# Two of four output projection tiles moved in among the next batch's score rounds

## The chip, the cores and the metric

One Trainium2 chip; the kernel is one program on one of its cores. The core has a matrix engine (TensorE, in the profile PE, with its weight loads as PEld), a vector engine (VectorE, DVE), an activation engine (ScalarE, ACT), a general engine (GpSimd, POOL) and a queue processor that here issues all transfers (SyncE, SP). Each runs its own list of instructions in order and waits on semaphores for the others. The metric is the device time of one execution in microseconds; lower is better.

## The reference

Eight batches of x, 512 tokens by 512 features. All are independent of one another.

```python
def reference(x, Wq, Wk, Wv, Wo, w_fc, w_proj):        # x: (8, 512, 512) float32
    xn = layernorm(x)                                  # eps 1e-5
    s = attention(xn)      # q, k, v = xn @ W.T in 16 heads of 32; rotary embedding on q and k;
                           # causal softmax(q k / sqrt(32)) v; then ctx @ Wo.T
    g = silu(ffn(xn))      # bitlinear(xn, w_fc) to 2048, exact gelu, bitlinear(., w_proj) to 512;
                           # bitlinear: layer norm, absmax rounding, weights made ternary
    return x + s * g
```

## The kernel before

Each batch is treated by `body(b)`, which every engine has in its own version. Tiles of 128 tokens or features; PSUM has eight banks of 128 x 512 float32. Values that need more than 16 bits are held as a high and a low part, so a product takes three matmuls (`three_products`), or two where the weights are ternary.

PE goes through one batch in this order:

1. v: 4 token tiles of 12 matmuls (L378).
2. q and k: 4 pairs of heads' halves, 24 matmuls each (L378). DVE multiplies by the rotary tables (L998) and adds (L1004), ACT rounds the sums to the high part (L724), POOL takes the low part (L1202), and SP copies the parts to the score operands, six transfers a pair (L304, `stacks`). This rotary part ends some time after PE's last q or k matmul. After the last of it SP issues the load of the next batch's x (L308, `load_next`). ACT then loads the table for Gelu (L738).
3. The output projection of the batch before, `out_projection(b - 1)` (L381): 4 token tiles of 12 matmuls, ctx times Wo, in banks 6 and 7 by turns. Tiles 2 and 3 wait until DVE has scaled tiles 0 and 1 out of these banks (`scale_by_gate`, L952, the instruction at L958). DVE runs all four scalings after its rotary work and before block 0 of the up projection. POOL adds x to the scaled tile (`add_x`, L1196): tiles 0 and 1 after its rotary work, tiles 2 and 3 after additions 8 and 11 of the squares (`RESIDUAL_AFTER`). SP stores each tile (L269).
4. The up projection: 16 blocks f of 8 matmuls (L493), in banks 1, 0, 2 by turns (`UP_BANKS`). Per block ACT does Gelu (L752), DVE two passes for the high and low part (L1047, L1049), and ACT the square (L747), which frees the bank. ACT's order is Gelu f, then square f - 1. PE's block f waits for square f - 3 (L488). After blocks 5, 7, 9 and 11 DVE takes the statistics of one tile of the next batch's x (`token_statistics`, L928), which first wait for x (L927). POOL sums the squares (L1211).
5. The score rounds, 44 of them (`ROUNDS`), whose only purpose is each row's maximum and sum: 16 of one head with 512 keys, 16 of one head with 384, then 12 for the short rows, 4 heads by 128 keys or 2 by 256. A round's scores and its mask (L472, L479) go to one of the five banks 3, 4, 5, 2, 1; DVE takes the maximum (L1025), POOL makes the bias for Exp from it (L1218; DVE the first four), ACT takes Exp and its sum (L778), after which the bank is free for the fifth round behind. In the short rows' rounds DVE also shifts and sums (L1033, L1039). Rounds 0 to 2 stand behind up blocks 13 to 15.
6. Between the rounds PE does the down projection step by step: a generator `down()` (L504) yields after each matmul (L524; beside nearly each stands a one-column sum, L523), in banks 6 and 7 by turns, 32 steps per token tile. How many steps have been given after round r is the list `DOWN_AFTER_ROUND`: 0, 0, 11, 13, 16 and then in proportion to ACT's work, 84 by round 43. Then come steps up to 104, the transposes of the maxima (L547) and more down steps. ACT copies down tiles 0 and 1 out of their banks after rounds 15 and 35 (`KEEP_DOWN`, L785).
7. The maxima's rows go to the score operand by a transfer (L315), for which the second set of scores (L578) waits; then Exp of them in transposed form (L799), the weighing by v (L609), and the transposes of the next batch's tokens (L399).

For batch 0 there is no output projection. That of the last batch is done at the end (`last_out_projection`), and the change doesn't touch it.

```python
while given < DOWN_AFTER_ROUND[r]:
    next(downs)
    given += 1
```

Of the kernel before, what the change touches and what calls it, by code (L numbers as in the profile page):

```python
# [12 lines left out]
P = 128  # L13
NB, S, D = 8, 512, 512
# [3 lines left out]
NT = S // P  # L18
# [4 lines left out]
NG = H // GH  # L23
# [14 lines left out]
NR = len(ROUNDS)  # L38
# [10 lines left out]
NSQ = len(SQ_SLOTS)  # L49
RESIDUAL_AFTER = {8: 2, 11: 3}  # L50
STATS_AFTER = (5, 7, 9, 11)
# [8 lines left out]
DOWN_LEAD = (0, 0, 11, 13, 16)  # L60
DOWN_AFTER_ROUND = [DOWN_LEAD[r] if r < NSB else DOWN_LEAD[-1] + (DOWN_BESIDE_SCORES - DOWN_LEAD[-1]) * EXP_COLS[r - NSB] // EXP_COLS[-1]
                    for r in range(NR)]
KEEP_DOWN = tuple(1 + min(r for r in range(NR) if DOWN_AFTER_ROUND[r] >= (t + 1) * DOWN_MATMULS) for t in range(2))
DOWN_BESIDE_EXP = 12
# [6 lines left out]
def program(nc, x, w_q, w_k, w_v, w_o, w_fc, w_proj, rope_cos, rope_sin, out, norm_row):  # L71
    with ExitStack() as ctx:
# [264 lines left out]
        def _(pe):  # L337
# [43 lines left out]
            def out_projection(b):  # L381
                for t in range(NT):
                    if t == 0:
                        pe.wait_ge(ctx_lo, b * NG + NG)
                    if t >= 2:
                        pe.wait_ge(scaled_ready, b * NT + t - 1)
                    three_products(banks[:, 6 + t % 2, :],
                                   lambda a, r, c: (ctxT[:, a, c, t * P:(t + 1) * P], voT[:, 1, r, c, :]),
                                   NG, "o").then_inc(wo_ps, 1)

            def turn_tokens(b, t, first=False):
# [27 lines left out]
            def body(b, first=False, last=False):  # L419
# [62 lines left out]
                for f in range(FC):  # L482
                    if f < 2:
                        pe.wait_ge(v_ready, b * NT + 3 + f)
                    elif f < NUB:
                        pe.wait_ge(rope_prod_ready, b * 16 + 12)
                    else:
                        pe.wait_ge(sq_ready, b * FC + f - NUB + 1)  # L488
# [15 lines left out]
                def down():  # L504
                    for t in range(NT):
                        if t == 0:
                            if not first:
                                pe.wait_ge(scaled_ready, b * NT)
                            pe.wait_ge(sq_ready, b * FC + FC - 2)
# [19 lines left out]
                if first:  # L529
                    ternary_row_sums()  # L530
                downs = down()
                given = 0

                for r in range(NR):
                    if r >= EARLY:
                        score_round(r)
                    while given < DOWN_AFTER_ROUND[r]:
                        next(downs)
                        given += 1
                while given < DOWN_BEFORE_MAXIMA:  # L540
                    next(downs)
                    given += 1
# [15 lines left out]
                mm.then_inc(sq_ps, 1)  # L558
                while given < NT * DOWN_MATMULS - DOWN_BESIDE_EXP:
                    next(downs)  # L560
                    given += 1
# [92 lines left out]
        def _(act):  # L654
# [53 lines left out]
            def body(b, first=False, last=False):  # L708
# [56 lines left out]
                for r, (i, h0, n) in enumerate(ROUNDS):  # L765
# [5 lines left out]
                    else:  # L771
# [9 lines left out]
                        mm.then_inc(sum_ready, 1)  # L781
                    if r in KEEP_DOWN:
                        t = KEEP_DOWN.index(r)
                        act.wait_ge(down_ps, b * NT + t + 1)
                        nc.scalar.copy(gate[:, t, :], banks[:, 6 + t % 2, :]).then_inc(down_kept, 1)  # L785
# [33 lines left out]
        def _(dve):  # L819
# [131 lines left out]

            def scale_by_gate(b, sums, final=False):  # L952
                dve.wait_ge(rope_sum_ready, sums)
                if final:
                    dve.wait_ge(gate_ready, b * NT + NT)
                for t in range(NT):
                    dve.wait_ge(wo_ps, b * NT + t + 1)
# [28 lines left out]
            def body(b, first=False, last=False):  # L986
# [26 lines left out]
                if not first:  # L1013
                    scale_by_gate(b - 1, b * 8 + 8)

# [44 lines left out]
                for r in range(EARLY, NR):  # L1060
                    maxima(r)
                dve.wait_ge(max_ready, b * NR + NR)
                split_parts(max_parts, row_max[:], -1.0, max_step, b * 3, max_split)
# [80 lines left out]
            body(NB - 1, last=True)  # L1144
            scale_by_gate(NB - 1, NB * 8, final=True)


        @block.gpsimd
        def _(pool):
# [48 lines left out]
            def body(b, first=False, last=False):  # L1198
# [8 lines left out]
                for f in range(1, FC):  # L1207
                    pool.wait_ge(sq_ready, b * FC + f + 1)
                    if f >= 2:
                        pool.wait_ge(sq_added, b * (FC - 1) + f - 1)  # L1210
                    nc.gpsimd.tensor_tensor(sq_sum[:], sq_sum[:], squares[f % NSQ], ALU.add).then_inc(sq_added, 1)  # L1211
                    if f in RESIDUAL_AFTER and not first:
                        add_x(b - 1, RESIDUAL_AFTER[f])

                for r in LONG[BIAS_DVE:]:
                    i, h0, n = ROUNDS[r]
                    pool.wait_ge(max_ready, b * NR + r + 1)
                    nc.gpsimd.tensor_scalar(exp_bias[:, i, h0:h0 + n], row_max[:, i, h0:h0 + n], col(EXP_SCALE), -1.0, ALU.mult, ALU.mult  # L1218
                                            ).then_inc(exp_bias_ready, 1)
                if not last:  # L1220
                    normalise(b + 1)
# [68 lines left out]
```

## Time and profile before

| | us |
|---|---|
| median of 3 runs | 1205.97 |
| lowest, highest | 1204.27, 1207.26 |
| the profiled execution | 1208.05 |
| its span, first to last instruction | 1206.2 |
| PE busy | 1157.1 |
| DVE busy | 851.2 |
| ACT busy | 787.0 |
| POOL busy | 522.0 |

The profile is one execution. Times in its rows are microseconds from the start of the span. A matmul's row gives start and length to its modelled end; the next one can start before that end, so how fast PE issues is read from starts. A timeline row with a count merges so many like instructions that follow one another, and the length runs from the first one's start to the last one's end. What stands in square brackets at a row's end is the idle time of the engine before it and what ended it.

### The profile page before, as it was taken

What the parts mean: (1) busy time and instruction counts of PE and PEld (TensorE: products, weight loads), DVE (VectorE), ACT (ScalarE), POOL (GpSimd) and SP (SyncE); (2) the same over time, 40 slices, a digit from 0 to 9 for tenths busy, and PEclk for the clock granted to TensorE, in tenths of its full rate; (3) what the DMA queues carried; (4) which work ended last, traced back from release to release, by engine and by line L of the source; (5) the groups of instructions that cost most, each with busy time, mean ns of one, the idle gap of its engine ahead of it and who ended that gap; (6) DMA issues with size and microseconds to landing.
All of it is one profiled execution on the core that took longest, in us unless ns stands there. A gap on an engine that the chain in (4) does not pass through costs nothing.

```text
span 1206.2 us, 19952 instructions
## 1 busy us (share of the span) xinstructions
PE 1157.1 (96%) x7580; PEld 562.3 (47%) x7580; DVE 851.2 (71%) x1445; ACT 787.0 (65%) x1486; POOL 522.0 (43%) x894
## 2 busy tenths in 40 slices
PE   4989999999999999999899999999989999999997
PEld 3555544445444454445444454444534445444553
DVE  7988948697457975588446985569735797557864
ACT  3687974487825977269561797438873487816974
POOL 2135361463525544363343635246352463526434
PEclk9999999999999999999899999999999999999999
DMA  8390011900137000550007401091011900146010
GB/s 296 149 117 26 1 28 50 161 19 2 28 39 136 19 4 26 78 115 1 26 4 85 108 2 29 1 155 38 3 28 17 158 19 2 27 55 95 9 38 36
DMA packets 52537, 67.30 MB, mean 56 GB/s; under 512 B 9304, under 2 KB 34264, under 8 KB 51928
## 3 DMA queue, kind: packets, MB, share of 16 engines
q1 hardware_dynamic: 52440, 66.01, 29.0%
q8 instruction: 60, 0.98, 0.4%
q14 instruction: 37, 0.30, 0.1%
HBM read 31.98 MB, written 8.40 MB: 33 GB/s over the span
## 4 chain that ended last, share of the span: by engine, by line
PE 60%; DVE 20%; ACT 15%; DMA 3%; issue 1%; SPq 1%; DVEq 0%; ACTq 0%
PE banks L378 24%; PE banks L524 9%; PE banks L493 9%; ACT banks L778 8%; PE banks L609 5%; PE banks L578 5%; DVE mix L1025 4%; ACT arena L799 4%; DVE arena L1049 4%; DVE arena L1047 4%; PE banks L472 2%; DMA stacks<-mix 2%; DVE banks L1033 1%; PE banks L399 1%; DVE mix L1039 1%; DVE mix L928 1%
## 5 line engine op out<-in xcount | busy, mean ns | idle before, releaser
L524 PE MATMUL banks<-projT,arena 128*128 128x512 f16 x1024 | 293.7, 380 | 0.0
L778 ACT ACTIVATE banks<-banks,mix,scl 128x512 f32<-128x512 f32 (+2 forms) x384 | 250.1, 698 | 4.5 <-POOL mix L1218 2.2
L1025 DVE TENSOR_REDUCE mix<-banks 128x1 f32<-128x384 f32 (+3 forms) x352 | 221.1, 639 | 28.7 <-PE banks L479 15.6
L493 PE MATMUL banks<-xT,fcT 128*128 128x512 f16 x1024 | 227.7, 379 | 0.1
L799 ACT ACTIVATE arena<-banks,scl 128x1280 f32<-128x1280 f32 x128 | 164.7, 1328 | 72.4 <-PE banks L578 69.3
L1211 POOL TENSOR_TENSOR xh_buf<-xh_buf 128x512 f32<-128x512 f32 x120 | 152.3, 1269 | 90.7 <-ACT xh_buf L747 86.5
L1202 POOL TENSOR_TENSOR split_buf<-xr_buf,split_buf 128x512 f16<-128x512 f32 x64 | 74.0, 1178 | 238.8 <-ACT split_buf L724 238.8
L378 PE MATMUL banks<-xT,qkT 128*128 128x512 f16 x768 | 168.7, 379 | 0.0
L1218 POOL TENSOR_SCALAR mix<-mix,scl 128x1 f32<-128x1 f32 (+1 forms) x288 | 76.3, 265 | 182.9 <-DVE mix L1025 182.3
L493 PEld LDWEIGHTS banks<-xT,fcT 128*128 128x128 f16 x1024 | 97.7, 98 | 120.1 <-ACT xh_buf L747 8.0
L1232 POOL TENSOR_SCALAR_AFFINE_SELECT arena<-arena 128x256 f32<-128x256 f32 x256 | 102.7, 428 | 90.0 <-ACT arena L799 90.0
L724 ACT CAST split_buf<-xr_buf 128x512 f16<-128x512 f32 x64 | 37.7, 617 | 158.6 <-DVE xr_buf L1004 80.6
L998 DVE TENSOR_TENSOR arena<-banks,mix 128x512 f32<-128x512 f32 x128 | 79.4, 682 | 85.1 <-PE banks L378 85.1
L752 ACT ACTIVATE banks<-banks,scl 128x512 f32<-128x512 f32 x128 | 84.8, 663 | 80.3 <-PE banks L493 80.1
L524 PEld LDWEIGHTS banks<-projT,arena 128*128 128x128 f16 x1024 | 98.5, 97 | 79.9 <-issue 1.7
L472 PE MATMUL banks<-stacks 96*128 96x128 f16 (+3 forms) x512 | 128.6, 302 | 6.3 <-ACT banks L778 2.1
L523 PE MATMUL banks<-ones,arena 128*128 128x1 f16 x768 | 126.0, 164 | 0.0
L378 PEld LDWEIGHTS banks<-xT,qkT 128*128 128x128 f16 x768 | 74.9, 98 | 87.8
L1047 DVE TENSOR_SCALAR arena<-banks,scl 128x512 f16<-128x512 f32 x128 | 95.2, 744 | 23.6 <-ACT banks L752 23.5
L578 PE MATMUL banks<-stacks 99*128 99x512 f16 (+3 forms) x512 | 93.7, 306 | 12.9 <-DMA stacks<-mix 8.9
L778 ACT ACTIVATION_READ_ACCUMULATOR banks<-banks,mix,scl 128x1 f32 x384 | 99.4, 259 | 0.0
L1049 DVE SCALAR_TENSOR_TENSOR arena<-banks,scl,arena 128x512 f16<-128x512 f32 x128 | 96.1, 751 | 4.5
(148 smaller groups left out, 1563.7 us busy)
## 6 DMA issues: line engine op xcount, KB each, us to landing
stacks<-split_buf SPq DMA_DIRECT2D x192, 128.0 KB, 5.5
xr_buf<-in_L_attn_x_dram SPq DMA_DIRECT2D x8, 1024.0 KB, 7.6
out_dram<-arena SPq DMA_DIRECT2D x32, 256.0 KB, 2.3
resid<-in_L_attn_x_dram SPq DMA_DIRECT2D x28, 256.0 KB, 6.8
stacks<-in_L_ffn_w_fc_dram SPq DMA_DIRECT2D x1, 4096.0 KB, 27.1
arena<-in_L_ffn_w_proj_dram SPq DMA_DIRECT2D x1, 4096.0 KB, 14.6
mix<-norm_row SPq DMA_DIRECT2D x8, 256.0 KB, 4.6
v_sb<-in_L_attn_Wv_dram SPq DMA_DIRECT2D x1, 1024.0 KB, 8.2
```

Source lines behind the costliest of these rows:

```text
L378: mm = pe.matmul(out_ap, lhs, rhs, start=(c == 0 and k == 0), stop=(c == n - 1 and k == 2))
L472: pe.matmul(bank[:, k * keys:(k + 1) * keys], q_stack[0:KS, h0 + k, i * P:(i + 1) * P], k_stack[0:KS, h0 + k, 0:keys], start=(k == 0), sto ...
L493: mm = pe.matmul(banks[:, UP_BANKS[f % NUB], :], fcT[:, c, f * P:(f + 1) * P], xT[:, part, c, :], start=(c == 0 and part == 0), stop=(c == ...
L523: pe.matmul(banks[:, 0, t:t + 1], lhs, ones16[:, 0:1], **ends)
L524: mm = pe.matmul(banks[:, 6 + t % 2, :], lhs, projT[:, f, :], **ends)
L578: mm = pe.matmul(ps[:, at:at + n], k_stack[0:KM, h, j * P:(j + 1) * P], q_stack[0:KM, h, j * P:S], start=True, stop=True)
L778: mm = nc.scalar.activation(block, block, ACT.Exp, scale=col(EXP_SCALE), bias=exp_bias[:, i, h0 + k:h0 + k + 1], accum_out=row_sum[:, i, h ...
L799: nc.scalar.activation(probs[:, g % 2, h % GH, :], st_region[(h + 1) % 2][:, 0:PROBS], ACT.Exp, scale=col(EXP_SCALE)).then_inc(probs_ready, 1)
L1025: nc.vector.tensor_reduce(row_max[:, i, h0:h0 + n], scores_of(r), AX_X, ALU.max).then_inc(max_ready, 1)
L1047: nc.vector.tensor_scalar(hid[:, 0, f, :], up, col(INV_G), None, ALU.mult).then_inc(hid_hi_ready, 1)
L1049: nc.vector.scalar_tensor_tensor(hid[:, 1, f, :], up, col(INV_G), hid[:, 0, f, :], ALU.mult, ALU.subtract).then_inc(hid_lo_ready, 1)
L1211: nc.gpsimd.tensor_tensor(sq_sum[:], sq_sum[:], squares[f % NSQ], ALU.add).then_inc(sq_added, 1)
```

## The change

Only output tiles 0 and 1 stay ahead of the up projection. Tiles 2 and 3 (24 matmuls) become steps of a generator, `late_out_projection`, which is chained ahead of `down()`. The schedule gives 120 steps in place of 96 by the same rule: 104 have been given by round 43, tile 2 is complete after round 3, tile 3 after round 8, down tile 0 is complete after round 22 and tile 1 after round 38. DVE scales tile 2 behind maximum 4 and tile 3 behind maximum 9 (`SCALED_AFTER`); POOL adds x to them behind the biases of rounds 6 and 11 (`RESIDUAL_AFTER`), no longer between the squares. Down tiles 0 and 1 wait for the scaling of tiles 2 and 3, whose banks they take. ACT copies down tiles 0 and 1 after rounds 23 and 39. Up blocks 0 and 1 exchange what they wait for of v. Batch 0 keeps the old numbers.

```diff
-RESIDUAL_AFTER = {8: 2, 11: 3}
+OUT_MATMULS = 3 * D // P
+OUT_EARLY = 2
+OUT_BESIDE_SCORES = (NT - OUT_EARLY) * OUT_MATMULS
...
+def given_after_rounds(total):
+    return [DOWN_LEAD[r] if r < NSB else DOWN_LEAD[-1] + (total - DOWN_LEAD[-1]) * EXP_COLS[r - NSB] // EXP_COLS[-1] for r in range(NR)]
...
+FIRST_GIVEN = given_after_rounds(DOWN_BESIDE_SCORES)
+GIVEN = given_after_rounds(OUT_BESIDE_SCORES + DOWN_BESIDE_SCORES)
+FIRST_KEEP_DOWN = tuple(round_behind(FIRST_GIVEN, (t + 1) * DOWN_MATMULS) for t in range(2))
+KEEP_DOWN = tuple(round_behind(GIVEN, OUT_BESIDE_SCORES + (t + 1) * DOWN_MATMULS) for t in range(2))
+SCALED_AFTER = {round_behind(GIVEN, (t + 1 - OUT_EARLY) * OUT_MATMULS): t for t in range(OUT_EARLY, NT)}
+RESIDUAL_AFTER = {r + 2: t for r, t in SCALED_AFTER.items()}
...
             def out_projection(b):
-                for t in range(NT):
+                for t in range(OUT_EARLY):
                     if t == 0:
                         pe.wait_ge(ctx_lo, b * NG + NG)
-                    if t >= 2:
-                        pe.wait_ge(scaled_ready, b * NT + t - 1)
...
+            def late_out_projection(b):
+                for t in range(OUT_EARLY, NT):
+                    pe.wait_ge(scaled_ready, b * NT + t - 1)
+                    for c in range(NG):
+                        for k, (a, r) in enumerate(((0, 0), (0, 1), (1, 0))):
+                            mm = pe.matmul(banks[:, 6 + t % 2, :], ctxT[:, a, c, t * P:(t + 1) * P], voT[:, 1, r, c, :],
+                                           start=(c == 0 and k == 0), stop=(c == NG - 1 and k == 2))
+                            if c == NG - 1 and k == 2:
+                                mm.then_inc(wo_ps, 1)
+                            yield
...
-                        pe.wait_ge(v_ready, b * NT + 3 + f)
+                        pe.wait_ge(v_ready, b * NT + 4 - f)
...
                     for t in range(NT):
+                        if t < 2 and not first:
+                            pe.wait_ge(scaled_ready, b * NT - 1 + t)
                         if t == 0:
-                            if not first:
-                                pe.wait_ge(scaled_ready, b * NT)
...
-                downs = down()
+                downs = itertools.chain(() if first else late_out_projection(b - 1), down())
+                ahead = 0 if first else OUT_BESIDE_SCORES
+                given_after = FIRST_GIVEN if first else GIVEN
...
-                    while given < DOWN_AFTER_ROUND[r]:
+                    while given < given_after[r]:
...
-                while given < DOWN_BEFORE_MAXIMA:
+                while given < ahead + DOWN_BEFORE_MAXIMA:
...
-                    scale_by_gate(b - 1, b * 8 + 8)
+                    scale_by_gate(b - 1, b * 8 + 8, range(OUT_EARLY))
...
                 for r in range(EARLY, NR):
                     maxima(r)
+                    if r in SCALED_AFTER and not first:
+                        scale_by_gate(b - 1, b * 8 + 8, (SCALED_AFTER[r],))
...
-                    if f in RESIDUAL_AFTER and not first:
-                        add_x(b - 1, RESIDUAL_AFTER[f])
...
+                    if r in RESIDUAL_AFTER and not first:
+                        add_x(b - 1, RESIDUAL_AFTER[r])
```

## Rows read from the trace of the kernel before

**Rows 1.** The page, busy us of each engine, share of the span, instructions

```profile
PE 1157.1 (96%) x7580; PEld 562.3 (47%) x7580; DVE 851.2 (71%) x1445; ACT 787.0 (65%) x1486; POOL 522.0 (43%) x894
```

**Rows 2.** PE's timeline, three batches: start, length, line, operation, names, shapes, count

```profile
227.96 1.24 PE L493 MATMUL banks<-xT,fcT 128*128 128x512 f16 x5
...
502.43 5.34 PE L378 MATMUL banks<-voT,ctxT 128*128 128x512 f16 x24
508.16 5.35 PE L378 MATMUL banks<-voT,ctxT 128*128 128x512 f16 x24 [0.39 <-DVE arena L958]
513.35 1.03 PE L493 MATMUL banks<-xT,fcT 128*128 128x512 f16 x4
...
949.73 1.46 PE L493 MATMUL banks<-xT,fcT 128*128 128x512 f16 x6
```

**Rows 3.** DVE's timeline in the up projection from 513.35

```profile
516.76 0.75 DVE L1049 SCALAR_TENSOR_TENSOR arena<-banks,scl,arena 128x512 f16<-128x512 f32 x1
...
526.06 0.69 DVE L928 BATCH_NORM_STATS2 mix<-xr_buf 128x6 f32<-128x512 f32 x1
...
527.43 0.75 DVE L1049 SCALAR_TENSOR_TENSOR arena<-banks,scl,arena 128x512 f16<-128x512 f32 x1
```

**Rows 4.** ACT's timeline around the same up projection

```profile
509.84 1.28 ACT L738 ACT_TABLE_LOAD   x1
515.28 0.66 ACT L752 ACTIVATE banks<-banks,scl 128x512 f32<-128x512 f32 x1 [4.16 <-PE banks L493]
...
528.21 0.69 ACT L747 ACTIVATE xh_buf<-banks,scl 128x512 f32<-128x512 f32 x1 [0.19 <-DVE arena L1049]
```

**Rows 5.** Windows: stretch, length, busy us (count) of PE, PEld, DVE, ACT, POOL, clock, DMA

```profile
541.96:581.50 39.54, 38.71 (x304) 20.66 (x302) 34.30 (x62) 38.00 (x106) 15.15 (x45) 1.00 0.01 1
...
589.60:596.30 6.70, 6.17 (x18) 2.55 (x19) 0.21 (x1) 2.65 (x2) 1.52 (x4) 0.50 0.00 0
```

**Rows 6.** PE in the score stage: two groups of 541.96 to 581.50, then the timeline

```profile
L524 PE MATMUL banks<-projT,arena 128*128 128x512 f16 x104 | 30.6, 376 | 0.0
L523 PE MATMUL banks<-ones,arena 128*128 128x1 f16 x96 | 15.8, 164 | 0.0
...
551.94 0.16 PE L523 MATMUL banks<-ones,arena 128*128 128x1 f16 x1
...
552.18 0.38 PE L472 MATMUL banks<-stacks 96*128 96x512 f16 x1
...
552.46 0.16 PE L523 MATMUL banks<-ones,arena 128*128 128x1 f16 x1
552.49 0.38 PE L524 MATMUL banks<-projT,arena 128*128 128x512 f16 x1
552.93 0.39 PE L472 MATMUL banks<-stacks 96*128 96x512 f16 x1
```

**Rows 7.** Waits of PE: who waited for whom, us in total, times, longest

```profile
PE banks L578 <- DMA stacks<-mix: 8.9, 3, 3.8
```

**Rows 8.** x loads of three batches: SP's issue, then KB and us to landing, in order

```profile
231.13 0.39 SPq L308 DMA_DIRECT2D xr_buf<-in_L_attn_x_dram  x1
515.51 0.59 SPq L308 DMA_DIRECT2D xr_buf<-in_L_attn_x_dram  x1
953.30 0.60 SPq L308 DMA_DIRECT2D xr_buf<-in_L_attn_x_dram  x1
...
xr_buf<-in_L_attn_x_dram SPq DMA_DIRECT2D x1, 1024.0 KB, 6.4
...
xr_buf<-in_L_attn_x_dram SPq DMA_DIRECT2D x1, 1024.0 KB, 8.0
...
xr_buf<-in_L_attn_x_dram SPq DMA_DIRECT2D x1, 1024.0 KB, 7.8
```

**Rows 9.** Timelines of POOL and ACT: the bias of round 5, and its Exp

```profile
547.64 0.26 POOL L1218 TENSOR_SCALAR mix<-mix,scl 128x1 f32<-128x1 f32 x1 [0.67 <-DVE mix L1025]
...
548.95 0.77 ACT L778 ACTIVATE banks<-banks,mix,scl 128x512 f32<-128x512 f32 x1
```

More of the change, by code:

```diff
@@ L1 @@
+import itertools
 from contextlib import ExitStack
@@ L60, with round_behind @@
 DOWN_LEAD = (0, 0, 11, 13, 16)
-DOWN_AFTER_ROUND = [DOWN_LEAD[r] if r < NSB else DOWN_LEAD[-1] + (DOWN_BESIDE_SCORES - DOWN_LEAD[-1]) * EXP_COLS[r - NSB] // EXP_COLS[-1]
-                    for r in range(NR)]
-KEEP_DOWN = tuple(1 + min(r for r in range(NR) if DOWN_AFTER_ROUND[r] >= (t + 1) * DOWN_MATMULS) for t in range(2))
+def given_after_rounds(total):
+    return [DOWN_LEAD[r] if r < NSB else DOWN_LEAD[-1] + (total - DOWN_LEAD[-1]) * EXP_COLS[r - NSB] // EXP_COLS[-1] for r in range(NR)]
+def round_behind(given, matmuls):
+    return 1 + min(r for r in range(NR) if given[r] >= matmuls)
+FIRST_GIVEN = given_after_rounds(DOWN_BESIDE_SCORES)
[4 more added lines that the diff above has]
+RESIDUAL_AFTER = {r + 2: t for r, t in SCALED_AFTER.items()}
 DOWN_BESIDE_EXP = 12
@@ L558, in body @@
                 mm.then_inc(sq_ps, 1)
-                while given < NT * DOWN_MATMULS - DOWN_BESIDE_EXP:
+                while given < ahead + NT * DOWN_MATMULS - DOWN_BESIDE_EXP:
                     next(downs)
@@ L781, in body @@
                         mm.then_inc(sum_ready, 1)
-                    if r in KEEP_DOWN:
-                        t = KEEP_DOWN.index(r)
+                    kept_down = FIRST_KEEP_DOWN if first else KEEP_DOWN
+                    if r in kept_down:
+                        t = kept_down.index(r)
                         act.wait_ge(down_ps, b * NT + t + 1)
@@ L950, in split_parts, with scale_by_gate @@
                 nc.vector.tensor_tensor(parts[:, :, 2, :], part_rest[:], parts[:, :, 1, :], ALU.subtract).then_inc(done, 1)
-            def scale_by_gate(b, sums, final=False):
+            def scale_by_gate(b, sums, tiles, final=False):
                 dve.wait_ge(rope_sum_ready, sums)
@@ L955, in scale_by_gate @@
                     dve.wait_ge(gate_ready, b * NT + NT)
-                for t in range(NT):
+                for t in tiles:
                     dve.wait_ge(wo_ps, b * NT + t + 1)
@@ L1144, in _ @@
             body(NB - 1, last=True)
-            scale_by_gate(NB - 1, NB * 8, final=True)
+            scale_by_gate(NB - 1, NB * 8, range(NT), final=True)
         @block.gpsimd
```

## Prediction

> **What bounds the kernel now.** I read the page's busy shares first: TensorE (PE) is busy 96% of the span, VectorE (DVE) 71%, ScalarE (ACT) 65%, GpSimd (POOL) 43% [rows 1]. The change neither adds nor removes a matmul; it permutes them. So the time can move only by PE's idle, and the question for each stage is where PE waits and what ends the wait. Since the busy shares take each matmul to its modelled end, which overlaps the next one's start, short idles don't show in them; I read them from starts instead. In the timeline of a steady batch (the batch whose up projection starts at 513.35) 24 matmuls of 512 columns take 5.34 us with the last one's 0.38, so one issues every (5.34 - 0.38)/23 = 0.2157 us [rows 2].
>
> Up projection: a group of 8 matmuls per block f, 1.73 us, and PE hardly waits. But it is tight: PE's group 9 would start at 513.35 + 9 x 1.726 = 528.88, and it needs the square of block 6, which ACT starts at 528.21 and ends 0.69 later, at 528.90 [rows 2, 4]. Slack: zero. That square waits for DVE's second pass over block 6 (527.43), which stands behind the token statistics at 526.06 [rows 3].
>
> Score stage, from the end of round 2 to the transposes of the maxima, 541.96 to 581.50: 39.54 us, in which ACT is busy 38.00 us [rows 5]. It holds 104 down matmuls (22.4 us at 0.2157), 96 one-column sums beside them (sum and matmul issue in 0.24 us, 551.94 to 552.18, so the sum takes 0.025, in all 2.4 us) and 41 rounds of 26,752 columns together; a round of 640 columns issues in 0.28 us (552.18 to 552.46), so these take 11.7 us [rows 6]. The sum is 36.5 us: PE idles about 3.0 us here. One such idle can be seen: 552.49 + 0.22 = 552.71, but the next round starts at 552.93, since its bank is still ACT's [rows 6].
>
> Behind the stage: PE waits at line 578 for the transfer of the maxima's rows three times, 8.9 us together, at most 3.8 [rows 7]. After the longest, the granted clock is 0.50, the 1.2 GHz level, from 589.6 to 596.3, where the rest stands at 1.00, 2.4 GHz [rows 5].
>
> **The change part by part.**
>
> *The move, ahead of the up projection.* Two tiles of 12 matmuls leave: 24 x 0.2157 = 5.18 us per batch, in 7 batches. Their own wait goes too: the second 24 start at 508.16, where 502.43 + 24 x 0.2157 = 507.61 was possible, and the releaser is the scaling of tile 0. But such a wait stands in this batch alone: 0.6 us in all [rows 2]. Call U the new start of the up projection, 5.2 us before the old (507.6 in this batch).
>
> *The same matmuls among the score rounds.* They come back as 24 steps ahead of the down steps. The schedule gives 104 of 120 steps with the rounds (84 of 96 before), and 24 instead of 20 remain ahead of the transposes. PE work of the stage becomes 36.5 + 5.2 = 41.7 us. ACT paces it now: by the schedule a round of 512 keys has 1.7 steps now and 2.3 afterwards, so PE's work for it rises from 0.28 + 1.7 x 0.24 = 0.69 us, below ACT's 0.75 or so, to 0.82, and PE hardly meets a taken bank. One new idle: rounds 3 and 4 come 0.3 us sooner, because 13 steps without a one-column sum stand ahead of them, and round 4's bank needs the last square, which the trace has only just in time: 0.3 us. With what is spread in nanoseconds I leave 0.5 us idle: the stage takes 42.2 us, 2.65 more, and 5.18 - 2.65 = 2.5 us is gained per batch, 17.7 us in seven; with the 0.6 above, **18.3 us**. Bounds: 0.6 (no idle filled) to 21.6 (all of it).
>
> *The cover that the move takes away.* Those 5.2 us of PE work lay beside ACT's, DVE's and SP's tail of the rotary part, which isn't moved.
> First, ACT. The table load for Gelu (1.28 us from 509.84) ends at 511.12, that is U + 3.5 [rows 4]. Before, Gelu of block 0 could follow PE (515.28, old start + 1.93) [rows 4]; now it starts at U + 3.5. From it to the end of block 0's square the before trace takes 2.99 us (Gelu 515.28, DVE's second pass 516.76, square 0.78 behind that and 0.69 long) [rows 3, 4]. So block 3, whose bank that is, starts at U + 6.55 instead of U + 5.18: 1.4 us idle.
> Second, the token statistics of the next batch. They wait for x, which SP issues at 515.51 and which lands 8.0 us later, 523.5 [rows 8]; this too stays tied to the rotary part. Before, that was 2.5 us before its use at 526.06. Now DVE gets there at 526.06 - 5.75 + 1.4 = 521.7 and waits 1.9 us. Behind it stand both passes of block 6, behind these ACT's square, and behind that PE's group 9, 2.9 us from the statistics by the starts above. So for group 9 only the landing counts: 523.6 + 2.9 = U + 18.9 against 15.6 when nothing waited: 3.3 us in all (the 1.4 is in it). The first and the last of the six batches with such a load: issued 231.13 and landed 6.4 later with the old start at 227.96, gives 9.6 + 5.2 + 2.95 - 15.6 = 2.1; 953.30 and 7.8 with 949.73 gives 11.4 + 5.2 + 2.95 - 15.6 = 3.9 [rows 2, 8]. Mean of the six, read so, 3.35, together 20.1; the seventh has no load and pays the ACT part, 1.4. Sum **21.5 us**. Bounds: 9.8 (the ACT part in seven batches, x always in time) to 26 (each landing 0.7 us later, near half of what the three shown differ by).
>
> *DVE's two scalings and POOL's two additions.* They go from the up projection into the rounds: two times 0.75 us on DVE behind maxima 4 and 9, two times 1.26 on POOL behind biases 6 and 11. Cover: DVE has a round's slack of 0.1 to 0.15 us, and POOL's bias for round 5 is there at 547.9, 1.0 us before ACT takes it [rows 9]. The scaling costs 0.7 of that for three or four rounds; the addition holds the bias of round 7 until about 550.5, when ACT wants it: nothing to 0.2 us on ACT, and PE, five banks ahead, doesn't see it. I take 0; if the cover is gone, 1 us a batch, 7 us.
>
> *Waits added on PE.* Late tile 2 and 3 wait for scalings that ended before the up projection; down tile 0 waits for the scaling behind maxima 4 (about 547.4), and PE's step 25 comes at about 549. Behind that wait the rounds are queued, but it is met. SP holds its stores of tiles 2 and 3 for 12 us longer; behind them stands only the transfer of the maxima's rows, near 582. The up projection's exchanged waits on v cost nothing: all v copies are far back. ACT's copy of down tile 1 moves from round 35 to 39, and the maxima's end has 1.6 us or more to spare.
>
> **Sum:** -18.3 + 21.5 = +3.2 us. The profiled execution took 1208.05 us (span 1206.2), 0.2% over the median of 1205.97; a difference carries over, so 1205.97 + 3.2, about 1209.2.
>
> The Trainium skill, "TensorE: Matmul & The Clock Gate", section "A second HAM failure mode: psum-queue depth-cycling", says that short idles between matmul groups that cycle through PSUM banks make the clock swing between its levels. The windows of this case show 1.00 over the whole score stage with its 3.0 us of such idles, so filling them gives back their time alone; by the page's rule more would be gained.
>
> **Rivals.**
> 1. *The waits in the up projection aren't paid* (other side). x lands in time: with SP's load 2 to 3 us sooner or DVE later than I reckon, only the ACT part stays: -18.3 + 9.8 = -8.5, 1197.5. For it: nothing in the landings (6.4 to 8.0 us); against: DVE's chain to block 5 is regular in every batch. It decides as faster where less than 14 us of the 21.5 are paid. 10%.
> 2. *The late landings of the maxima's rows go or come.* 8.9 us of waiting and, by the stretch at 0.50 and a shorter one in a second batch, some 4.7 us of slow clock are in the trace before, with the three such waits, while PE's cover there doesn't change. If they don't recur: 3.2 - 13.6 = -10.4, 1195.6. As many more of them would be +13. 12% for gone, 5% for more.
> 3. *The clock falls at the new idles.* An idle of 3.8 us was followed by the 1.2 GHz level. The new ones are 1.4 and about 2, at most 2.6 us. A stretch of 3.4 us at half clock, half of the one shown, costs 1.7 us; at each of six it makes 1205.97 + 3.2 + 10.2 = 1219.4. Against: the shorter waits at line 578 left no such stretch. 12%. The page named above, section "Why this matters for your kernels", also warns of long idle gaps as the cause of a fall.
> 4. *ACT starves in the rounds*, which it fills: DVE's 1.5 and POOL's 2.5 us more there delay it by 1 us per batch: 3.2 + 7, 1216.2. 12%.
>
> **How the numbers follow.** Forecast 49%, its own range 1205 to 1213, since each of its two sums can be off by 3 us. 0.3% of 1206 is 3.6 us, about what a measurement can tell from no change, so the boundaries are 1202.4 and 1209.6; the forecast stands right beneath the upper one and gives 22% slower, 25% same, 2% faster. With rivals 1 and 2 (22%, of them 18 faster, 4 same), 3, 4 and more late landings (29%, of them 24 slower, 5 same): faster 0.20, same 0.34, slower 0.46. The range from 1198 to 1218 leaves out most of rival 2's good end and the clock's bad one.
>
> **What the profile after would show.** Right: up groups 0 to 2, then an idle of 1.4 us ended by ACT's square; a second before group 9, with DVE idle ahead of the statistics until x lands; a score stage of some 42.2 us with hardly an idle of PE and ACT no longer full. Wrong: statistics that don't wait; stretches at 0.50 inside the up projection; ACT waiting for POOL's bias of rounds 7 or 12; a number of waits at line 578 other than three.

## The result, and the profile after

| | us |
|---|---|
| before, median of 5 runs | 1205.97 (1203.73 to 1207.26) |
| after, median of 5 runs | 1215.16 (1213.16 to 1217.89) |
| ratio, 95% interval | 1.0084 (1.0059 to 1.0109) |
| after, the profiled execution | 1214.59, span 1212.8 (before 1208.05, 1206.2) |

Slower by 0.84% by the ratio, and by 9.2 us in these medians. The forecast was 1209.2 in a range from 1198 to 1218; the measured time lies in the range, but above the 1205 to 1213 that the prediction gave to the forecast itself.

Three of the things that PE waits for, over the whole span (who waited for whom, us in total, times, longest):

```profile
PE banks L518 <- ACT xh_buf L774: 19.7, 12, 3.2
...
PE banks L605 <- DMA stacks<-mix: 12.3, 3, 4.2
...
PE banks L497 <- ACT banks L805: 0.3, 1, 0.3
```

L518 is the up projection, which before did not appear in this list; L605 is the old L578 [rows 7], whose wait has grown. The waits of the score rounds for ACT's banks (L497), 2.1 us in 8 before, have nearly gone.

The fourth batch in PE's timeline, after:

```profile
505.23 5.34 PE L394 MATMUL banks<-voT,ctxT 128*128 128x512 f16 x24
510.41 5.34 PE L518 MATMUL banks<-xT,fcT 128*128 128x512 f16 x24
517.31 10.53 PE L518 MATMUL banks<-xT,fcT 128*128 128x512 f16 x48 [1.56 <-ACT xh_buf L774]
529.39 1.90 PE L518 MATMUL banks<-xT,fcT 128*128 128x512 f16 x8 [1.55 <-ACT xh_buf L774]
```

Where one unbroken run of up matmuls stood, three groups of 8 are followed by an idle and six more by a second one. From the starts (24 matmuls take 5.18) the first is 517.31 - 515.59 = 1.72 us, the second, before group 9, 1.7. Both end with an ACT square. Behind the squares stand these rows of ACT and DVE:

```profile
513.00 1.28 ACT L765 ACT_TABLE_LOAD   x1
514.30 1.24 ACT L779 ACTIVATE banks<-banks,scl 128x512 f32<-128x512 f32 x2
516.57 0.69 ACT L774 ACTIVATE xh_buf<-banks,scl 128x512 f32<-128x512 f32 x1 [1.03 <-DVE arena L1077]
```

```profile
524.18 0.75 DVE L1077 SCALAR_TENSOR_TENSOR arena<-banks,scl,arena 128x512 f16<-128x512 f32 x1
526.48 0.69 DVE L956 BATCH_NORM_STATS2 mix<-xr_buf 128x6 f32<-128x512 f32 x1 [1.55 <-DMA xr_buf<-in_L_attn_x_dram]
527.10 0.73 DVE L1075 TENSOR_SCALAR arena<-banks,scl 128x512 f16<-128x512 f32 x1
527.87 0.75 DVE L1077 SCALAR_TENSOR_TENSOR arena<-banks,scl,arena 128x512 f16<-128x512 f32 x1
```

The table load ends 3.9 us after the up projection has begun (before: 2.2 us ahead of it [rows 4]), and Gelu follows at once. The token statistics, which waited for nothing before [rows 3], wait for x. From 526.48 to group 9 at 529.39 are 2.9 us, as before.

The score stage, from round 2's end to the transposes of the maxima (L574, the old L547), as the windows and the timeline give it:

```profile
542.41:584.43 42.02, 41.89 (x329) 22.65 (x327) 35.20 (x64) 38.14 (x106) 18.45 (x50) 1.00 0.04 14
```

```profile
584.42 0.40 PE L574 MATMUL banks<-ident,mix 128*48 128x128 f16 x4
...
586.47 2.75 PE L549 MATMUL banks<-projT,arena 128*128 128x512 f16 x12
593.39 0.74 PE L605 MATMUL banks<-stacks 99*128 99x512 f16 x4 [4.17 <-DMA stacks<-mix]
```

It is 42.02 - 39.54 = 2.48 us longer than before [rows 5] and holds 24 matmuls, 5.18 us, more: 2.70 us of idle a batch have been filled, 18.9 us in seven. The granted clock stands at 1.00 over the whole stage in both kernels, so filling these short idles gave back their own time and no more. The same view shows the wait for the maxima's rows, 4.2 us where it was 3.8, and behind it again a stretch at the 1.2 GHz level:

```profile
594.00:597.30 3.30, 3.30 (x11) 1.40 (x10) 0.00 (x0) 1.68 (x2) 0.78 (x2) 0.50 0.00 0
```

**The account of the two profiled executions.** Filled idle: -18.9. The scaling's wait: -0.6. Idles before group 3 (0.17, 2.14, 1.72, 1.33, 1.37, 1.52 and 1.48 us in the seven batches, 9.7) and before group 9 (1.27, 0.91, 1.71, 2.26, 3.32 and 2.63, 12.1), less the 0.4 us at group 9 that stood there before: +21.4. Waits for the maxima's rows: 12.3 - 8.9 = +3.4. Clock: ahead of the last microseconds, 10.2 us ran at half clock before and 13.7 after; half of the difference is +1.7. Sum +7.0; the spans differ by 6.6.

### The profile page after: what moved, and what is told of

Same layout as the page of the kernel before. It is cut to its first block, busy times and chain, and to the rows that moved or that the text cites. A ratio compares the mean times of both kernels' runs of the same rounds, so it can differ in the third digit from the quotient of the medians.

```text
span 1212.8 us, 19966 instructions
## 1 busy us (share of the span) xinstructions
PE 1146.7 (95%) x7580; PEld 560.5 (46%) x7580; DVE 846.3 (70%) x1445; ACT 788.1 (65%) x1486; POOL 521.3 (43%) x894
## 4 chain that ended last, share of the span: by engine, by line
PE 58%; DVE 15%; DMA 11%; ACT 7%; SPq 4%; POOL 2%; issue 2%; DVEq 0%; ACTq 0%; POOLq 0%
PE banks L549 18%; PE banks L394 13%; PE banks L497 5%; PE banks L636 5%; PE banks L605 5%; DMA stacks<-split_buf 5%; ACT arena L827 4%; SPq L320 4%; DMA xr_buf<-in_L_attn_x_dram 4%; DVE arena L1077 4%; PE banks L518 3%; DVE arena L1075 3%; POOL split_buf L1232 2%; PE banks L504 2%; DMA stacks<-mix 2%; DVE arena L1026 2%
## 5 line engine op out<-in xcount | busy, mean ns | idle before, releaser
L549 PE MATMUL banks<-projT,arena 128*128 128x512 f16 x1024 | 289.2, 381 | 0.0
L518 PE MATMUL banks<-xT,fcT 128*128 128x512 f16 x1024 | 229.5, 379 | 19.8 <-ACT xh_buf L774 19.7
L518 PEld LDWEIGHTS banks<-xT,fcT 128*128 128x128 f16 x1024 | 97.1, 98 | 142.2 <-ACT xh_buf L774 31.7
L497 PE MATMUL banks<-stacks 96*128 96x128 f16 (+3 forms) x512 | 127.5, 299 | 1.4 <-ACT banks L805 0.3
L605 PE MATMUL banks<-stacks 99*128 99x512 f16 (+3 forms) x512 | 94.2, 308 | 16.4 <-DMA stacks<-mix 12.3
L774 ACT ACTIVATE xh_buf<-banks,scl 128x512 f32<-128x512 f32 x128 | 87.5, 684 | 27.2 <-DVE arena L1077 23.6
```

The costliest lines, as they stand in the source:

```text
L497: pe.matmul(bank[:, k * keys:(k + 1) * keys], q_stack[0:KS, h0 + k, i * P:(i + 1) * P], k_stack[0:KS, h0 + k, 0:keys], start=(k == 0), sto ...
L518: mm = pe.matmul(banks[:, UP_BANKS[f % NUB], :], fcT[:, c, f * P:(f + 1) * P], xT[:, part, c, :], start=(c == 0 and part == 0), stop=(c == ...
L549: mm = pe.matmul(banks[:, 6 + t % 2, :], lhs, projT[:, f, :], **ends)
L605: mm = pe.matmul(ps[:, at:at + n], k_stack[0:KM, h, j * P:(j + 1) * P], q_stack[0:KM, h, j * P:S], start=True, stop=True)
```

## The experiments

Each is compared with the kernel before, which ran on the same chip. The runs were made in four sets, the last three on three different chips. The kernel before took 1205.97, 1209.11, 1209.3 and 1205.31 us in them, so a difference of two medians out of different sets is uncertain by some 4 us. "The changed kernel" is the one with the change of this case. Batches are numbered from 0 where a number stands for them: the fourth batch is batch 3.

**The load of x sooner.**

```diff
                     sp.wait_ge(rot_lo_ready, b * 8 + 2 * pair + 2)
+                    if pair == 3 and not last:
+                        sp.dma_start(x_sb, x[b + 1].rearrange("(t p) d -> p t d", p=P)).then_inc(x_dma, 16)
...
-                if not last:
-                    load_next()
```

> The changed kernel, with SP's load of the next x issued ahead of the last pair's six transfers to the score operands, 3.9 us sooner. Theory A (the new time is lost to two waits of the up projection, for ACT's tail and for x): the idle before group 9 (1.27, 0.91, 1.71, 2.26, 3.32 and 2.63 us, 12.1 in all) goes, the one before group 3 stays; about 1203 us, 0.997 of the kernel before. Theory B (the additions on DVE and POOL starve ACT in the rounds, and the idle before group 9 is taken up by slack elsewhere): stays near 1215, 1.008. Theory C (more or longer late landings of the maxima's rows are the loss): stays near 1215 too, with the waits for them at three times 4 us.

Measured: 1204.24 us, ratio 0.9958 (0.9943 to 0.9974). PE's timeline of the fourth batch and its waits:

```profile
509.60 5.34 PE L515 MATMUL banks<-xT,fcT 128*128 128x512 f16 x24
516.53 14.74 PE L515 MATMUL banks<-xT,fcT 128*128 128x512 f16 x67 [1.59 <-ACT xh_buf L771]
```

```profile
PE banks L602 <- DMA stacks<-mix: 12.5, 3, 4.5
PE banks L515 <- ACT xh_buf L771: 9.1, 6, 2.6
```

The idle before group 9 is gone (12 waits of 19.7 us became 6 of 9.1), the one before group 3 stands. The waits for the maxima's rows are what they were, so these can't be the loss that this edit gave back. Theory A holds; B and C expected no gain.

**The table load sooner.**

```diff
+                    if pair == 3:
+                        nc.scalar.preload_act_table(ACT.Gelu)
                     split_rotated(pair)
...
-                nc.scalar.preload_act_table(ACT.Gelu)
+                if first:
+                    nc.scalar.preload_act_table(ACT.Gelu)
```

> The changed kernel, with the table load for Gelu ahead of the last pair's two roundings on ACT, where ACT waits anyway, in all batches but the first. Theory A: Gelu of block 0 starts 1.28 us sooner, so the idle before group 3 falls from 2.14, 1.72, 1.33, 1.37, 1.52, 1.48 to 0.9, 0.4, 0.1, 0.1, 0.2, 0.2 and goes in the first such batch. But in the six batches with a load of x the idle before group 9 grows by as much, since the landing alone sets that group; so only the last batch gains, 1.3 us: about 1214, 1.007. A theory in which the two waits add up independently would give 1.28 x 7, 1207.

Measured: 1223.45 us, ratio 1.0112 (1.0089 to 1.0136). The medians put this run 8 us above the changed kernel, the profiled spans 10.4 us; by the ratios, 1.0112 for 1.0084, the intervals overlap. No theory had it slower. The first idle is nearly gone, and the second has grown by it, as expected. But see what follows it. PE's timeline and a window of the fifth batch:

```profile
664.04 15.84 PE L518 MATMUL banks<-xT,fcT 128*128 128x512 f16 x72
683.60 8.75 PE L518 MATMUL banks<-xT,fcT 128*128 128x512 f16 x28 [3.73 <-ACT xh_buf L777]
```

```profile
682.00:688.70 6.70, 5.10 (x13) 1.79 (x14) 4.96 (x8) 3.19 (x5) 2.65 (x3) 0.50 0.08 30
```

Nine groups run without a stop, then one idle of 3.9 us stands where two of 1.3 and 2.3 were, and with it the clock falls to 1.2 GHz for 6.8 us. In this execution 41 us ran at half clock ahead of the last microseconds, against 13.7 in the changed kernel's; half of the difference, 13.6 us, is more than the 10.4 us between their spans. So here two short idles were cheaper than one long. It isn't a matter of length alone: of these idles one of 2.3 us and one of 2.85 had such a stretch with them and one of 2.83 didn't, nor had the 3.3 us one of the changed kernel.

**Both.**

> The changed kernel with both: the load of x sooner and the table load sooner. Theory A: both idles go but for some 2 us in all, about 19 us of the 21.5 are back: 1196, 0.991 of the kernel before; the score stage stays 42.5 us long, with its idle filled. Theories B and C: 1215.

Measured: 1194.47 us, ratio 0.9873 (0.9851 to 0.9894), a little better than expected. The waits of PE begin so; the up projection's are 0.7 us in all, the score stages are 42.52 us long, counted from the last up matmul:

```profile
PE banks L372 <- DVE w_all L850: 13.3, 2, 11.6
PE banks L602 <- DMA stacks<-mix: 12.9, 3, 4.5
```

So the pair gives back some 21 us by the medians, 25 by the ratios, and the load of x is the edit without which the other brings nothing.

**Both, on the kernel before.**

> Control: the kernel before with both the load of x and the table load sooner. There neither x nor ACT is waited for in the up projection (x lands 1.3 to 3.1 us before its use), so by theory A nothing changes: 1206, 1.000. If it gains as much as the changed kernel does, the cures act on something else.

Measured: 1205.89 us, ratio 0.9975 (0.9956 to 0.9994). Nearly nothing, as expected; the 0.25% I can't place: up and score stages are to 0.1 us those of before, and the runs of both scatter by 9 us.

**The norms' transfers later.** In all traces so far the waits for the maxima's rows stood in batches 1, 3 and 5. There PE goes on 5.6 to 8.0 us after the issue (before and after), in the other batches 3.8, without a wait. SP issues the four transfers of the norms (4 bytes per element) 1.0 us behind, in the kernels with late tiles 0.8 us.

The packets of the rows themselves are not late. The DMA view of the kernel before, over the first 2.5 us from the issue (582.46 to 584.96, where PE went on 7.7 us after the issue, and 730.86 to 733.36, where it went on after 3.8):

```profile
DMA packets 318, 0.05 MB, mean 20 GB/s; under 512 B 270, under 2 KB 318, under 8 KB 318
...
DMA packets 317, 0.05 MB, mean 20 GB/s; under 512 B 269, under 2 KB 317, under 8 KB 317
```

In either there are 48 packets of 1 KB, the whole 48 KB of the rows, among 4-byte packets of the norms. So what PE gets late is the word that the transfer is complete; "late landing" means this here.

```diff
                 sp.dma_start(q_stack[KS:KM, :, :], maxT[:, :]).then_inc(max_dma, 16)
                 if not last:
+                    sp.wait_ge(max_dma, b * 16 + 16)
                     spread_norms(b + 1)
```

> The changed kernel; SP waits for the landing of the maxima's rows before it issues the four small transfers of the next batch's norms, which it otherwise issues 1 us behind them. The waits for the maxima's rows stand in batches 1, 3 and 5 in every trace so far, 8.9 us in the kernel before and 12.3 in the changed one. Theory D (the small transfers behind them on the same rings hold up the last part of the landing): the three waits go, with the stretches at 0.50 behind them, 12.3 + 6.8 us less: about 1196, 0.990. Theory E (the landing is late for another reason): three waits of 4 us stay and the time stays at 1.008, or worse by what the norms then come late.

> The kernel before with the same wait on SP. Theory D: its 8.9 us of waits and some 5 us of half clock go: 0.988. Then the changed kernel against the kernel before, both so cured, is 1.002 to 1.004, the 3.2 us of the prediction; what was beyond it is the longer wait for the maxima's rows. Theory E: 1.000.

Measured: the changed kernel 1198.51 us, 0.9907 (0.9885 to 0.993); the kernel before 1194.11 us, 0.9874 (0.9853 to 0.9895). SP's queue of the kernel before with this edit, and the waits of PE in both, the changed kernel's last:

```profile
580.36 0.78 SPq L315 DMA_DIRECT2D stacks<-mix  x1
584.03 1.75 SPq L277 DMA_DIRECT2D norm_row<-norm_c  x4
```

```profile
PE banks L360 <- DVE w_all L823: 13.7, 2, 11.9
PE banks L579 <- ACT arena L800: 3.5, 8, 0.4
```

```profile
PE banks L519 <- ACT xh_buf L775: 20.3, 11, 3.3
PE banks L376 <- DVE w_all L851: 13.9, 2, 12.0
```

The wait for the maxima's rows is gone from both, and in the kernel before so is every stretch at half clock ahead of the last microseconds. Theory D is shown as far as the edit goes: the late landings need the small transfers behind them. These don't cause one every time: in four of the seven batches that have them there is none, and in the last run below batch 3 has none either. Between the two kernels so treated stands the change by itself: 1198.51 - 1194.11 = 4.4 us, where the prediction's sum was 3.2. It isn't free of the clock: the changed kernel's profiled execution has two stretches of 3.4 us at half clock in the up projection, at idles of 2.6 us, and the kernel before none. Half of their length, 3.4 us, is what they cost of the 5.1 us between the two spans.

**The late matmuls left out.** Two of the 24 stay, in `late_out_projection`:

```diff
-                            mm = pe.matmul(banks[:, 6 + t % 2, :], ctxT[:, a, c, t * P:(t + 1) * P], voT[:, 1, r, c, :],
-                                           start=(c == 0 and k == 0), stop=(c == NG - 1 and k == 2))
                             if c == NG - 1 and k == 2:
-                                mm.then_inc(wo_ps, 1)
+                                pe.matmul(banks[:, 6 + t % 2, :], ctxT[:, a, c, t * P:(t + 1) * P], voT[:, 1, r, c, :],
+                                          start=True, stop=True).then_inc(wo_ps, 1)
                             yield
```

> The changed kernel without 22 of the 24 late output matmuls: of tiles 2 and 3 only the last matmul is done (this part of the computation is left out, the steps of the schedule stay). If the matmuls really fill idle of PE, taking 22 x 0.2157 = 4.7 us of them per batch away shortens the score stage by 2.2 us only, from 42.5 to 40.3 or so (ACT ends it): 1215 - 15.5, about 1200, 0.995. If the stage is PE's own throughout, it shortens by 4.7 us a batch: 1182.

Measured: 1226.39 us, ratio 1.0142 (1.0119 to 1.0166). Less work and more time, 1.4% above the kernel before where the changed kernel is 0.8% above it (10.2 us between the two spans): my expectation overlooked that the matmuls left out are the cover of rounds 3 and 4. PE's timeline there, and the window behind:

```profile
546.84 0.38 PE L496 MATMUL banks<-stacks 96*128 96x512 f16 x1
547.06 0.22 PE L503 MATMUL banks<-mask_q,ident 128*128 128x128 bf16 x1
548.45 0.38 PE L496 MATMUL banks<-stacks 96*128 96x512 f16 x1 [1.17 <-ACT xh_buf L773]
548.66 0.22 PE L503 MATMUL banks<-mask_q,ident 128*128 128x128 bf16 x1
548.72 0.38 PE L411 MATMUL banks<-voT,ctxT 128*128 128x512 f16 x1
550.59 0.58 PE L496 MATMUL banks<-stacks 96*128 96x512 f16 x1 [1.49 <-ACT xh_buf L773]
```

```profile
549.90:556.60 6.70, 5.87 (x20) 1.85 (x21) 6.02 (x13) 6.62 (x17) 3.87 (x8) 0.50 0.03 12
```

Rounds 3 and 4 each wait for their bank's last square, and the clock falls, for 3.4 or 6.8 us in each of the seven batches. As a measure of the filled idle the run says nothing; it shows what the matmuls ahead of these rounds are worth.

**One late tile.** `OUT_EARLY = 3`; tile 2 ahead again waits for the scaling of tile 0, and POOL adds x to it behind square 8.

> The changed kernel with three output tiles ahead of the up projection and one late (12 matmuls moved, cover taken 2.6 us). Theory A: the ACT part is covered but for batch 2, group 9 waits for x some 2.6 us less, 0 to 2 us a batch, 6 us in all against 21.5; the score stage grows by 0.5 us instead of 2.5, so nearly all of 2.6 us of idle a batch is filled by one tile already, 14 us. Sum -8 and the waits for the maxima's rows as in the changed kernel, +5: 1203, 0.997.

Measured: 1205.83 us, ratio 0.997 (0.9955 to 0.9985). That is 3 us above the expectation; the waits for the maxima's rows are 14.0 us here, not the 12.3 that it counted on. The up projection's waits, and the two ends of the fourth batch's score stage:

```profile
PE banks L520 <- ACT xh_buf L776: 5.0, 4, 1.5
```

```profile
541.92 0.59 PE L412 MATMUL banks<-voT,ctxT 128*128 128x512 f16 x2
...
582.14 0.40 PE L576 MATMUL banks<-ident,mix 128*48 128x128 f16 x4
```

The stage takes 40.22 us: 0.68 more for 2.59 us of matmuls. The first tile fills 1.9 us of idle, the second 2.70 - 1.91 = 0.8, and it is the second that brings most of the idle in the up projection (5.8 us in all with one late tile, 21.8 with two, from starts): with one late tile the move is a small gain, 0.3%.

**All three edits, with two late tiles, on the kernel before, and with one late tile.**

> The changed kernel with the load of x and the table load sooner and with SP's wait for the maxima's rows ahead of the norms. Theory A with D: nothing of the three losses is left; 1194.5 less 12.9 us of waits for the maxima's rows and 8.5 us of half clock behind them gives 1173, 0.970. Against the kernel before with the same three edits (next run) that is 1.7%, 20 us: 18.9 us of filled idle and 0.6 us of the scaling's wait.

> The kernel before with the same three edits. By theories A and D the first two do nothing here and the third all: 1194, 0.987, as with the third alone. If the difference to the run before this one is less than 15 us, the filled idle of the score stage is not worth what I take it for.

> Three output tiles ahead, one late, with the three edits. One late tile fills 1.9 us of the stage's idle, the second 0.8 more. So this should be 7 x 0.8 = 5.6 us slower than with two late, less 0.9 us for what is left of ACT's tail in batch 2: about 1178, 0.974. If it is the faster one, the second tile's fill is paid for elsewhere.

Measured: two late tiles 1175.46 us, 0.974 (0.971 to 0.9771); the kernel before 1194.2 us, 0.9895 (0.9857 to 0.9932); one late tile 1180.89 us, 0.9783 (0.9752 to 0.9814). PE's waits in the first of these:

```profile
PE banks L373 <- DVE w_all L851: 13.6, 2, 11.8
PE banks L603 <- ACT arena L828: 3.5, 8, 0.4
...
PE banks L516 <- ACT xh_buf L775: 1.3, 2, 1.0
```

With next to nothing left of the losses (1.3 us of waits in the up projection) the move is worth 1194.2 - 1175.46 = 18.7 us, 1.6%, against 19.5 from the filled idle and the scaling's wait. The second tile is worth 5.4 of it.

**Tile 3's matmuls left out.** As above, but only for tile 3: 11 of its 12 matmuls.

```diff
+                            if t == NT - 1 and not (c == NG - 1 and k == 2):
+                                yield
+                                continue
...
-                                           start=(c == 0 and k == 0), stop=(c == NG - 1 and k == 2))
+                                           start=(c == 0 and k == 0) or t == NT - 1, stop=(c == NG - 1 and k == 2))
```

> The changed kernel without 11 of the 12 matmuls of late tile 3 (left out of the computation; the steps stay, so rounds 3 and 4 keep all their cover and rounds 4 to 8 get less). If idle is what the moved matmuls fill, ACT holds rounds 5 to 9 back by the same 2.4 us and the score stage stays at 42.4 us; if PE's work alone counts, it is 40.1. In tiles_left_out the cover of rounds 3 and 4 went too, and the stage became longer.

One run, 1222.7 us. The fall of the clock spoils five of the seven stages here too (0.50 from 701.0 to 704.3 inside one); the third batch's stage ran undisturbed:

```profile
405.30 0.81 PE L413 MATMUL banks<-voT,ctxT 128*128 128x512 f16 x3
...
447.13 0.40 PE L577 MATMUL banks<-ident,mix 128*48 128x128 f16 x4
```

```profile
405.30:447.10 41.80, 40.19 (x317) 21.52 (x315) 35.08 (x64) 38.17 (x106) 18.45 (x50) 1.00 0.04 14
```

41.83 us against 42.02: taking 2.37 us of matmuls away shortens the stage by 0.19. (The expectation's 42.4 counts from the last up matmul, 0.5 us sooner; so counted this is 42.33.) The eighth batch's, undisturbed too, is shorter by the same 0.19 (41.70 for 41.89). The early rounds go at ACT's pace or nearly so, and what PE does beside them is free. In the batches with the clock's fall the stage took 43.6 to 44.0, counted from the last up matmul. The wait for the maxima's rows is missing in batch 3 of this run, with the small transfers 0.8 us behind as ever.

The same 12 matmuls seem to cost 0.19 us here and 1.8 in the run with one late tile (42.02 - 40.22). The runs differ in the schedule. Here its 120 steps stay where they were; with one late tile it has 108, so all rounds have fewer, and so has the stretch behind the last round. That stretch, from the last mask to the transposes, in the kernel before and after:

```profile
576.20 0.27 PE L479 MATMUL banks<-mask_q,ident 128*128 128x256 bf16 x1
...
581.50 0.40 PE L547 MATMUL banks<-ident,mix 128*48 128x128 f16 x4
```

```profile
578.16 0.27 PE L504 MATMUL banks<-mask_q,ident 128*128 128x256 bf16 x1
```

It takes 5.30 us before, 5.79 with one late tile and 6.26 with two (584.42 - 578.16), for 20, 22 and 24 steps, in which PE has no idle to fill. So 0.96 of the 2.48 us by which the stage grew are four steps more behind the last round. Whether giving them beside the early rounds would save this time wasn't tried.

## Why the prediction was right, and where it was short

The way was right, the measured time lies in the range, and the two terms of the sum hold. The size was short: the sum said +3.2 us, and the medians moved by 9.2. What it lacked are terms that it put at nothing, the late landings and the clock.

*The filled idle* was put at 2.5 us a batch and measured 2.70. 18.3 us were forecast with the scaling's wait, and 18.7 came out once nothing else was in the way. What idle is left in the stage is as small as reckoned: 42.02 us for 41.7 of PE's work, where 0.5 was allowed.

*The cover taken away* was put at 21.5 us and is 21.4: ACT's tail before group 3, x before group 9, the latter set by the landing alone. Nor do only the sums agree: for batches 1, 3 and 6 the prediction had 2.1, 3.3 and 3.9 us, and 1.4, 3.4 and 4.2 were measured. That the two waits don't add is shown by the table load's edit, which only moved idle from one to the other, and that x is the cause of the second by the edit on its load.

*The additions on DVE and POOL* cost nothing. ACT did wait more for POOL's biases, 6.0 us in 22 waits against 2.2 in 8, but the new ones stand 24 us and more behind a batch's first Exp, far from rounds 7 and 12, and PE's waits for ACT's banks fell to 0.3 us. Rival 4 falls; with all three edits the move gains 18.7 us with these additions in it.

*The late landings.* The term that was mis-sized is the one left at nothing: rival 2 had "PE's cover there doesn't change", and gave more of them 5% only. They stood in the same three batches, but each was longer: 12.3 us together for 8.9, and 3.4 us more ran at half clock, which cost 1.7. These 5.1 us are more than what the profiled execution has beyond the forecast, 6.6 - 3.2 = 3.4. It was written as a matter of chance, while it is one of order on SP's queue, as the edit showed. Why the waits are longer with late tiles (12.3 to 14.0 us in the six such traces with three waits, 8.9 and 9.8 in the two without late tiles) wasn't tried. One difference is on record: with late tiles the first small transfer is issued 0.8 us behind the rows, without them 1.0.

*The clock.* Rival 3 happened, though not in the changed kernel's profiled execution but near by: in that with the norms later, stretches at half clock stand at idles of 2.6 us in two batches. Its ground for being unlikely was a misreading: the prediction says that the shorter waits at line 578 left no such stretch, but of its three waits (1.8, 3.8 and 3.3 us) only the one of 1.8 left none; that of 3.3 us had one of 3.4 us. The remaining 2 to 3 us between the medians' 9.2 and the spans' 6.6 may be such stretches in other executions. The mean granted clocks point that way, 0.990 to 0.993 in the four other executions of the changed kernel against 0.994 in the profiled one, but one of the four was the shortest of all; it is argued, not shown.

What each of SP's four small transfers does to the landing ahead of them, and why most batches escape, stays open. The Trainium skill, "DMA: Bandwidth & Descriptors", section "Queues, rings and completion order", says that a transfer's increment of its semaphore lands only after every earlier write of the same DMA engine, across its queues. It names nothing that transfers issued later would do to it. The runs show that such transfers can matter: with the four transfers 1 us behind it PE waited 8.9 us in three batches of the kernel before, with them behind its landing not at all. The first 4-byte packets start 1.9 us after the issue of the rows, whose own last packets end at 2.4; whether they count as earlier writes no run here shows.

## What to carry to other kernels

Work moved off a place where the bound engine covers others' tails must be paid there: list what was hidden (a table load, a load whose issue is tied to another queue) and move these first. Here that was the load of x, two lines. With the other two edits added, the same move turned from 0.8% slower to 1.6% faster against the kernel before with the same edits. Waits in series behind one late arrival don't add, so curing the first alone brings nothing, and made one long idle out of two short ones, with a lower clock on top. Keep small transfers that are not yet needed behind the landing of one that the bound engine needs. And look at what a longer schedule puts behind its last filler place: those steps cost their full time.

## What the runs showed of the hardware that I had not expected

- With the table load sooner, one idle of 3.6 to 4.5 us of PE had the 1.2 GHz level with it for 3.4 to 6.8 us in each of three batches. Left-out matmuls made a kernel slower, by waits of 1.2 and 1.5 us that lie 2 us apart and the clock's fall with them (0.50 from 549.9 to 556.6). Idles of 2.3 to 2.9 us had it at times, one of 3.3 us had not.
- PE could go on 3.8 us after the issue of a transfer of three rows in some batches and 5.6 to 8.8 in others, though its 48 packets were over 2.4 us after the issue in both. With four transfers of 4-byte elements held back until it had landed (issue 580.36, the others from 584.03) PE went on after 3.7 to 3.9 us in all batches.
- An edit of one wait on SP, on the kernel before, is worth 1.3% by itself (ratio 0.9874); with the two other edits, which do nearly nothing there, the ratio is 0.9895.
